# Attention: the bf16 parts of q and k are made on GpSimd, and a later group's preparation moves one tile

## The chip, the cores and the metric

The kernel runs on one core of a Trainium2 chip. The metric is the device time of one execution in microseconds (us), smaller is better. The engines are named as in the profile: PE (TensorE), DVE (VectorE), ACT (ScalarE), POOL (GpSimd) and SP, whose queue issues the DMAs.

## The reference, cut to what matters

A residual stream x of 32 tiles (128 tokens by 128 features) goes through four pairs of gated attention and gated feed-forward. Three attentions (layers 0, 1 and 3) have projections, 16 heads of width 8, and keys and values from a context of the same shape:

```python
x = x + tanh(g_xattn[0]) * L0_xattn(layernorm(x), ctx, ctx, mask, Wq, bq, Wk, bk, Wv, bv)
x = x + tanh(g_ffn[0]) * L0_ffn(layernorm(x), weight, bias)          # fp8 of x and of weight
x = x + tanh(g_xattn[1]) * L1_xattn(layernorm(x), ctx, ctx, Wq, Wk, Wv, bv, Wo, bo)
x = x + tanh(g_ffn[1]) * L1_ffn(...)                                  # 8 experts, top 2
x = x + tanh(g_xattn[2]) * L2_xattn(layernorm(x), ctx, ctx)           # 16 x 16 heads per token
x = x + tanh(g_ffn[2]) * L2_ffn(...)
x = x + tanh(g_xattn[3]) * L3_xattn(layernorm(x), ctx, ctx, mask, Wq, bq, Wk, bk, Wv, bv, Wo, bo)
x = x + tanh(g_ffn[3]) * L3_ffn(...)                                  # 8 experts, top 2
# each of L0, L1 and L3_xattn, for every tile and head:
scores = q @ k.T * 8 ** -0.5      # masked
out = softmax(scores) @ v
```

## The kernel before, in words

The 32 tiles are eight groups of four. The program has seven stages: attention 0, feed-forward 0, attention 1, feed-forward 1 with the per-token attention of layer 2, feed-forward 2, attention 2 (which is layer 3's), feed-forward 3. Every engine has its own instruction list, written out by hand in program order; semaphores (`wait_ge`) order the engines. The function `walk` unrolls the first two and the last two groups and loops over the four between.

**A group's preparation in an attention.** DVE takes the layer norm's statistics of the group's four tiles (`norm_stats`, L1171 and L1176). POOL makes the inverse deviation (`inv_std`, L447 and L449). DVE applies it (`norm`, L1194) and writes `xn`. PE turns `xn` (`turn_xn`, L815) and ACT takes it from PSUM (`take_xnT`, L635). PE then projects q, k and v one after the other through the same bank X_BANK (`project` 1 and 2, L824, and 3, L828); ACT takes q and k into the SBUF tile `area` (`take_q`, L641, and `take_k`, L646), and DVE takes v (`take_v`, L1205).

**The split.** The scores are computed with bf16 matmuls, so q and k (together 128 x 1024 fp32) are split into three bf16 parts: copy to bf16, subtract, copy, subtract, copy (`split`, L1233, L1235, L1230). The last of the five signals `split_ready`.

**The spread.** SP waits for `split_ready` and issues 18 DMAs (`spread`: six at L355 to `q_rows`, twelve at L359 to `k_rows`) that put the parts of each head onto the partitions that the matmuls contract over. `q_rows` and `k_rows` are double, by the parity of the group. After a spread SP issues the load of a later group's context (L341) and, in attention 0, of its mask (L347). The next split overwrites the parts, so it waits until the spread before it has landed (`rows_spread`).

**A tile's work.** While tile n is worked on, the scores of tile n + 1 are computed (`scores`, L845 and L847) and DVE reduces them to row maxima (`head_max`, L1220; `split_max`, L1242 and L1244). PE turns the maxima (`turn_max`, L857), computes the transposed scores less the maximum (`scores_t`, L866, L868, L873), ACT exponentiates them (L662), and PE weighs the values (`weigh`, L885). DVE normalises tile n - 1 (`normalise`, L1251, L1253, and L1256 in attention 0; `add_out`, L1261 and L1265, in the others). PE's list for tile n begins with the first scores of tile n + 1, so at the last tile of a group it begins with those of the next group, which wait for that group's spread:

```python
if j == 0:
    pe.wait_ge(rows_spread, REP * (G0[a] + group_of[0] + 1))
```

**Where the preparation of group gr + 2 stands**, while group gr with tiles t = 0 to 3 is worked on: statistics and normalising at the end of t = 0; `turn_xn` and `take_xnT` at the end of t = 1; q, then k, at t = 2; v at t = 3; and the split on DVE at t = 3, its parts between the four `head_max`. v is taken by DVE, and the mask converted, at t = 1 of the next group. In attention 0 DVE also takes the statistics of a finished group at the end of t = 2 and normalises it for feed-forward 0 at the end of t = 3 (`normed`, L1183 and L1187). Groups 0 and 1 are prepared in a start part: for attention 0 at the beginning of the kernel, for attentions 1 and 2 after the first two groups of feed-forward 0 and 2. The split of group 0 stands in it; that of group 1 stands on DVE after the first tile's maxima.

POOL has little to do in the attentions (`inv_std` only). In feed-forward 2 it also finishes the per-token products (`products`, L546, and `weighted`, L559).

## Time and profile before

| | |
|---|---|
| runs, median of 3 (lowest, highest) | 1914.92 us (1913.74, 1922.96) |
| profiled execution, span | 1906.2 us |
| between the span and the median of the runs | 8.7 us |
| mean granted TensorE clock | 0.933 of full speed |
| PE, DVE, ACT, POOL busy | 83%, 73%, 36%, 27% |

The profile gives its execution's span, from the first to the last instruction, and no other time of its own; the 8.7 us outside the span belong to every run. Sums below are made against the span and carried to the median. The two levels of TensorE's clock are 2.4 GHz (granted 1.0) and 1.2 GHz (0.5).

### The profile page before, as it was taken

To read this page: it belongs to the slowest core of one execution; us is meant where nothing else is said; L and a number is where in the kernel's file an instruction comes from. 1 tells how busy PE (TensorE), PEld (TensorE's weight loads), DVE (VectorE), ACT (ScalarE), POOL (GpSimd) and SP (SyncE) were. 2 spreads that over 40 slices of the span, in tenths; PEclk is the share of its full clock that TensorE was granted. 3 is DMA by queue.
4 is the path that set the end of the run, shared out by engine and by line. 5 is a ranking of instruction groups with operands and counts; after the bars stand their busy time and mean duration, and the time that the engine had idled before them with its cause. 6 is when DMAs were issued, how large, how long until landed. Compare 5 with 4: busy or idle time off the path is not lost. (4 is left out here: it accounts for less than half of the span.)

```text
span 1906.2 us, 36266 instructions
## 1 busy us (share of the span) xinstructions
PE 1579.4 (83%) x12360; PEld 997.5 (52%) x12360; DVE 1396.8 (73%) x3603; ACT 684.9 (36%) x1218; POOL 521.0 (27%) x565
## 2 busy tenths in 40 slices
PE   3889895388999899889889899935699899787787
PEld 1556563156666556555455555522466666444454
DVE  5777776666676446887888888876567666599997
ACT  1344443134444322333333433412344444333332
POOL 2000000000000002453543453553000000478786
PEclk9999997589999899999999999965999999899998
DMA  6453540244335000000000000004052432000000
GB/s 145 63 72 46 74 59 1 34 134 65 54 53 68 3 1 1 6 1 7 1 6 6 0 7 17 1 0 72 11 68 41 65 52 35 1 1 12 11 12 12
DMA packets 62745, 62.68 MB, mean 33 GB/s; under 512 B 6032, under 2 KB 57744, under 8 KB 62096
## 3 DMA queue, kind: packets, MB, share of 16 engines
q1 hardware_dynamic: 62608, 60.94, 20.1%
q8 instruction: 75, 1.23, 0.3%
q14 instruction: 62, 0.51, 0.1%
HBM read 21.07 MB, written 2.10 MB: 12 GB/s over the span
## 5 line engine op out<-in xcount | busy, mean ns | idle before, releaser
L662 ACT ACTIVATE probs<-bank 128x512 f32<-128x512 f32 x384 | 229.4, 598 | 357.8 <-PE bank L873 351.5
L1220 DVE TENSOR_REDUCE neg_max<-bank 128x4 f32<-128x512 f32 x384 | 260.1, 687 | 123.1 <-PE bank L847 117.5
L1020 PEld LDWEIGHTS bank<-room,area 128*128 128x128 f32 x2048 | 249.3, 195 | 102.7 <-issue 62.5
L447 POOL TENSOR_SCALAR rstd_a<-meanvar 128x4 f32<-128x4 f32 x64 | 17.0, 265 | 1042.9 <-DVE meanvar L1176 1042.9
L1020 PE MATMUL bank<-room,area 128*128 128x128 f32 x2048 | 259.5, 281 | 33.5 <-DVE area L1501 19.0
L737 ACT ACTIVATE work<-bank 128x512 f32<-128x512 f32 (+1 forms) x192 | 114.6, 597 | 356.2 <-PE bank L1045 351.2
L1049 PE MATMUL bank<-xT,room 128*128 128x512 f32 (+1 forms) x384 | 200.5, 604 | 15.5 <-DVE area L1501 15.3
L845 PE MATMUL bank<-mask_b,ident_b 128*128 128x512 bf16 x384 | 153.4, 399 | 62.7 <-DVE neg_max L1220 50.4
L1045 PE MATMUL bank<-xT,room 128*128 128x512 f32 (+1 forms) x384 | 199.2, 601 | 0.0
L1501 DVE TENSOR_TENSOR area<-work,bank 128x512 f32<-128x512 f32 (+1 forms) x192 | 128.7, 679 | 95.7 <-PE bank L1049 75.8
L559 POOL TENSOR_TENSOR prod<-mask_i,work 128x128 f32<-128x128 f32 (+3 forms) x128 | 126.5, 1021 | 155.1 <-DVE mask_i L1562 155.1
L868 PE MATMUL bank<-q_rows,k_rows 128*128 128x128 bf16 x1536 | 152.1, 223 | 0.0
L873 PE MATMUL bank<-neg_max_t,pick_max 128*128 128x128 bf16 x1536 | 151.7, 222 | 0.0
L847 PE MATMUL bank<-k_rows,q_rows 128*128 128x256 bf16 x768 | 151.6, 280 | 0.0
L868 PEld LDWEIGHTS bank<-q_rows,k_rows 128*128 128x128 bf16 x1536 | 121.2, 100 | 57.3 <-issue 10.2
L885 PE MATMUL bank<-probs,v_aug 128*32 128x128 f32 x3072 | 149.8, 287 | 1.0 <-ACT probs L662 0.7
L866 PE MATMUL bank<-ident_b,mask_b 128*128 128x512 bf16 x384 | 149.4, 389 | 0.0
L1472 DVE SCALAR_TENSOR_TENSOR x<-bank,comb,x 128x128 f32<-128x128 f32 (+1 forms) x512 | 143.0, 339 | 5.6 <-PE bank L1020 3.5
L546 POOL TENSOR_TENSOR probs<-h,work 128x128 f32<-128x128 f32 (+3 forms) x128 | 114.4, 924 | 83.1 <-DVE probs L1542 73.8
L1049 PEld LDWEIGHTS bank<-xT,room 128*128 128x128 f32 (+1 forms) x384 | 68.8, 183 | 118.0 <-issue 86.8
L1194 DVE TENSOR_SCALAR xn<-x,meanvar,rstd 128x128 f32<-128x128 f32 (+1 forms) x192 | 76.8, 463 | 57.3 <-POOL rstd L449 57.2
L873 PEld LDWEIGHTS bank<-neg_max_t,pick_max 128*128 128x128 bf16 x1536 | 104.6, 100 | 0.0
(172 smaller groups left out, 2499.8 us busy)
## 6 DMA issues: line engine op xcount, KB each, us to landing
q_rows<-area SPq DMA_DIRECT2D x144, 128.0 KB
k_rows<-area SPq DMA_DIRECT2D x288, 64.0 KB
ctxT<-ctx_t SPq DMA_DIRECT2D x24, 256.0 KB, 8.4
mask_i<-mask SPq DMA_DIRECT2D x8, 256.0 KB, 8.4
work<-ctx_in SPq DMA_DIRECT2D x8, 256.0 KB, 2.8
out<-x SPq DMA_DIRECT2D x4, 512.0 KB, 3.2
room<-w_down SPq DMA_DIRECT2D x1, 1536.0 KB, 13.7
room<-w_gate SPq DMA_DIRECT2D x1, 1408.0 KB, 6.2
```

The costliest lines, as they stand in the source:

```text
L662: act.activation(probs[j].rearrange("p a b -> p (a b)"), T_BANK[j % 2][:], ACT.Exp).then_inc(exp_done, 1)
L845: pe.matmul(dst[:], ident_b[:], bcast(mask(b, t), 4), start=True, stop=False)
L847: mm = pe.matmul(dst[:, 256 * i:256 * i + 256], q_rows[b][:, 2 * j + i, tok], k_rows[b][:, :, 2 * j + i, tok], start=False, stop=i == 1)
L866: pe.matmul(dst[:], mask(b, t), bcast(ident_b[:], 4), start=True, stop=False)
L868: pe.matmul(dst[:, i * P:(i + 1) * P], k_rows[b][:, i % 2, 2 * j + i // 2, tok], q_rows[b][:, 2 * j + i // 2, tok], start=False, stop=False)
L873: mm = pe.matmul(dst[:, i * P:(i + 1) * P], pick_max[:, 4 * j + i, :], neg_max_t[t % 2][:], start=False, stop=i == 3)
L885: mm = pe.matmul(O_BANK[32 * i:32 * i + 32, j * P:(j + 1) * P], v_aug[b][:, t, 4 * j + i, :], probs[j][:, i, :], start=True, stop=True)
L1020: mm = pe.matmul(dst[:, t * P:(t + 1) * P], h[:, t * P:(t + 1) * P], w, start=i == 0, stop=i == len(terms) - 1)
L1045: pe.matmul(S_BANK[(3 * e + c) % 2][0:size, :], wg[:, e, at:at + size], xT[b][:], start=True, stop=True).then_inc(gate_filled, 1)
L1049: pe.matmul(T_BANK[(3 * e + c) % 2][0:size, :], wu[:, e, at:at + size], xT[b][:], start=True, stop=True).then_inc(up_filled, 1)
L1220: dve.tensor_reduce(neg_max[:, 4 * j:4 * j + 4], S_BANK[j % 2][:].rearrange("p (h k) -> p h k", h=4), AX.X, ALU.max, negate=True).then_inc ...
L1472: ins = dve.scalar_tensor_tensor(xt, src[:, t * P:(t + 1) * P], comb[cb][:, t, e:e + 1], xt, ALU.mult, ALU.add)
```

## The change

DVE's `split` goes; POOL gets one of the same five instructions, with the same two waits ahead of it. On POOL the split of group 0 stands in the start part, that of group 1 directly behind (so ahead of the first tile), and that of group gr + 2 after the `inv_std` of its statistics. For attention 2 the split of group 0 stands in POOL's feed-forward 2 between the last `products` and the last two `weighted`.

The preparation of group gr + 2 stays in order but stands later: statistics still at the end of t = 0; normalising at the end of t = 1; `turn_xn`, `take_xnT` and q at t = 2; k and v at t = 3, k in the tile's first half. In attention 0 the statistics and the normalising for feed-forward 0 stand one tile earlier than before.

```diff
+            def split(p, a):
+
+                pool.wait_ge(prep_read, 4 * (G0[a] + p) + 3)
+                if positive(REP * (G0[a] + p)):
+                    pool.wait_ge(rows_spread, REP * (G0[a] + p))
+                for part in range(2):
+                    src = qk if part == 0 else qk_rest
+                    waits_apart(pool)
+                    pool.tensor_copy(parts[:, :, part, :], src).then_inc(pool_steps, ch.one())
+                    pool.wait_ge(pool_steps, ch.count)
+                    pool.tensor_tensor(qk_rest, src, parts[:, :, part, :], ALU.subtract).then_inc(pool_steps, ch.one())
+                    pool.wait_ge(pool_steps, ch.count)
+                waits_apart(pool)
+                pool.tensor_copy(parts[:, :, 2, :], qk_rest).then_inc(split_ready, 1)
+
             def attention0():
                 inv_std(1)
                 inv_std(2)
+                split(0, 0)
                 pool.wait_ge(quant_steps, 1)
...
+                split(1, 0)
...
             def attention(a):
+                split(1, a)
+
                 def body(gp, first, last, a=a):
                     for gr, b, _, left in groups(gp, first, last):
                         if left >= 2:
                             inv_std(L0[a] + gr + 3)
+                            split(gr + 2, a)
...
                 products(last + 3, 3, 1)
+                split(0, 2)
                 weighted(last + 2, 2, 1)
...
# ACT
                             exp(n, 1)
                             if left >= 2 and t == 2:
-                                take_q(gr + 2)
+                                take_xnT(gr + 2)
+                            if left >= 2 and t == 3:
+                                take_k(gr + 2)
                             exp(n, 2)
...
                             exp(n, 3)
-                            if left >= 2 and t == 1:
-                                take_xnT(gr + 2)
                             if left >= 2 and t == 2:
-                                take_k(gr + 2)
+                                take_q(gr + 2)
...
# PE
                             if left >= 2 and t == 2:
-                                project(gr + 2, b, 1)
+                                turn_xn(gr + 2)
                             if left >= 2 and t == 3:
-                                project(gr + 2, b, 3)
+                                project(gr + 2, b, 2)
                             scores_t(n, b, t, 0)
...
                             scores_t(n, b, t, 3)
-                            if left >= 2 and t == 1:
-                                turn_xn(gr + 2)
                             if left >= 2 and t == 2:
-                                project(gr + 2, b, 2)
+                                project(gr + 2, b, 1)
+                            if left >= 2 and t == 3:
+                                project(gr + 2, b, 3)
...
# DVE
-                            if splits:
-                                split(gr + 2, 0)
...
                             if t == 0 and left >= 2:
                                 norm_stats(gr + 2, xc - NT + TG * (gr + 3), x_written if a else x_loaded)
+                            if t == 1 and left >= 2:
                                 dve.wait_ge(prep_filled, 4 * (G0[a] + gr + 1) + 1)
                                 norm(gr + 2, L0[a] + gr + 2 if a or (first and b == 0) else 2 * gr + 1)
                             if a == 0 and not is_first_group(first, b):
                                 norm_count = 2 * gr + 2 if not last else 13 + b
+                                if t == 1:
+                                    norm_stats(gr - 1, TG * gr)
                                 if t == 2:
-                                    norm_stats(gr - 1, TG * gr)
-                                if t == 3:
                                     normed(gr - 1, norm_count)
```

## Rows read from the trace of the kernel before

**Rows 1.** The page: busy time, share of the span, instructions of each engine.

```profile
PE 1579.4 (83%) x12360; PEld 997.5 (52%) x12360; DVE 1396.8 (73%) x3603; ACT 684.9 (36%) x1218; POOL 521.0 (27%) x565
```

**Rows 2.** Windows, attention 0, tiles t = 0 to 3 of one group, bounded by turn_max.

```profile
core 0: us, PE busy (x) PEld busy (x) DVE busy (x) ACT busy (x) POOL busy (x), PEclk, DMA share, GB/s
120.68:127.46 6.78, 6.72 (x85) 4.44 (x86) 6.42 (x18) 3.15 (x6) 0.00 (x0) 1.00 0.74 104
127.46:138.16 10.70, 8.53 (x97) 5.71 (x89) 6.75 (x22) 3.62 (x7) 1.27 (x2) 0.84 0.80 96
138.16:146.40 8.24, 8.24 (x97) 5.06 (x89) 4.68 (x15) 4.40 (x8) 0.00 (x0) 1.00 0.28 49
146.40:154.87 8.47, 7.66 (x102) 5.18 (x93) 7.74 (x17) 3.13 (x6) 1.27 (x2) 1.00 0.01 4
```

**Rows 3.** Timeline of DVE at the end of t = 0, attention 0.

```profile
129.81 1.12 DVE L1194 TENSOR_SCALAR xn<-x,meanvar,rstd 128x128 f32 x4 [1.55 <-POOL rstd L449]
```

**Rows 4.** Windows from t = 3 of group 0 to t = 3 of group 6, attentions 0, 1, 2.

```profile
78.85:279.20 200.35, 183.17 (x2136) 119.98 (x2128) 149.23 (x392) 84.06 (x159) 15.04 (x22) 0.96 0.46 64
420.62:620.60 199.98, 185.13 (x2209) 127.08 (x2200) 139.59 (x337) 88.58 (x183) 6.33 (x10) 0.98 0.43 58
1400.29:1599.15 198.86, 184.94 (x2208) 127.06 (x2200) 139.26 (x337) 88.46 (x183) 6.33 (x10) 0.98 0.41 55
```

**Rows 5.** Timeline of SP and PE, attention 0, spread of group 7 and its first use.

```profile
258.08 3.80 SPq L355 DMA_DIRECT2D q_rows<-area  x6
261.92 7.88 SPq L359 DMA_DIRECT2D k_rows<-area  x12
...
278.22 0.38 PE L845 MATMUL bank<-mask_b,ident_b 128*128 128x512 bf16 x1 [1.70 <-issue]
```

**Rows 6.** Timeline of PE: turn_max at t = 3 of groups 5 and 6.

```profile
249.18 0.22 PE L857 MATMUL bank<-ident_b,neg_max_parts 128*32 128x128 bf16 x1
...
279.20 0.22 PE L857 MATMUL bank<-ident_b,neg_max_parts 128*32 128x128 bf16 x1
```

**Rows 7.** Timeline of SP and PE, attention 0, spread of group 0.

```profile
26.05 3.91 SPq L355 DMA_DIRECT2D q_rows<-area  x6
...
45.90 0.61 PE L845 MATMUL bank<-mask_b,ident_b 128*128 128x512 bf16 x1 [9.64 <-DMA k_rows<-area]
```

**Rows 8.** Timeline of PE and ACT: start of t = 2, and its take_q.

```profile
137.17 0.38 PE L845 MATMUL bank<-mask_b,ident_b 128*128 128x512 bf16 x1
...
141.64 0.68 ACT L641 ACTIVATE area<-bank,bq_s 128x512 f32<-128x512 f32 x1
```

**Rows 9.** Groups by line and form, DVE: the split.

```profile
L1235 DVE TENSOR_TENSOR area<-area 128x1024 f32<-128x1024 f32 x48 | 59.7, 1245 | 1.7
...
L1233 DVE CAST area<-area 128x1024 bf16<-128x1024 f32 x48 | 33.6, 701 | 7.1 <-ACT area L646 6.9
...
L1230 DVE CAST area<-area 128x1024 bf16<-128x1024 f32 x24 | 16.5, 687 | 0.2
```

**Rows 10.** Groups by line and form, POOL.

```profile
L484 POOL TENSOR_TENSOR probs<-probs,work 128x512 f32<-128x512 f32 x64 | 82.6, 1291 | 48.8 <-DVE probs L1630 48.8
...
L546 POOL TENSOR_TENSOR probs<-h,work 128x512 f32<-128x512 f32 x32 | 41.4, 1293 | 0.0
...
L546 POOL TENSOR_TENSOR probs<-h,work 128x128 f32<-128x128 f32 x32 | 18.9, 590 | 83.1 <-DVE probs L1542 73.8 <-DVE h L1194 9.3
...
L436 POOL TENSOR_SCALAR_AFFINE_SELECT pick_max<-pick_max 128x2048 bf16<-128x2048 bf16 x2 | 4.0, 2010 | 0.6 <-POOL pick_max L432 0.5
```

**Rows 11.** Timeline of POOL and DVE, start part of attention 2.

```profile
1285.93 3.81 POOL L559 TENSOR_TENSOR prod<-mask_i,work 128x128 f32<-128x128 f32 x4
...
1286.07 3.77 DVE L1194 TENSOR_SCALAR xn<-x,meanvar,rstd 128x128 f32<-128x128 f32 x4 [1.62 <-POOL rstd L449]
```

**Rows 12.** Timeline of POOL and DVE, start part of attention 2, last tokens.

```profile
1306.57 3.83 POOL L559 TENSOR_TENSOR prod<-mask_i,work 128x128 f32<-128x128 f32 x4 [4.95 <-DVE mask_i L1562]
...
1310.43 1.67 DVE L1568 TENSOR_REDUCE mask_i<-prod 128x32 f32<-128x128 f32 x4 [3.34 <-POOL prod L559]
```

**Rows 13.** Timeline of DVE, feed-forward 0 behind the start part of attention 1.

```profile
361.95 0.69 DVE L1367 TENSOR_TENSOR qb<-work 128x512 bf16<-128x512 f32 x1 [6.12 <-PE bank L986]
```

More of the change, by code:

```diff
@@ L467, in body @@
                             inv_std(count)
-                walk(pool, body, ch, 4)
+                        if not last:
+                            split(gp + b + 2, 0)
+                walk(pool, body, ch, 12)
             def attention(a):
+                split(1, a)
                 def body(gp, first, last, a=a):
@@ L537, in feed_forward0 @@
                 inv_std(18)
+                split(0, 1)
             def products(n, t, b):
@@ L1281, in attention @@
                         take_mask(0, 0)
-                    for part in range(3):
-                        split(0, part)
                     if a == 0:
@@ L1301, in attention @@
                 split_max(0)
-                for part in range(3):
-                    split(1, part)
                 def body(gp, first, last, a=a, xc=xc):
@@ L1325, in body @@
                                 head_max(n + 1, 2)
-                            if splits:
-                                split(gr + 2, 1)
                             if has_next:
@@ L1330, in body @@
                                 split_max(n + 1)
-                            if splits:
-                                split(gr + 2, 2)
                             if has_prev and a > 0:
@@ L1658 @@
 PHASES = 7
-DVE_PER_TRIP = (32, 26, 26)
+DVE_PER_TRIP = (24, 18, 18)
 def laid_out(i):
```

16 lines of the change are left out of this document (1 added, 15 removed).

## The prediction

> **What bounds the kernel now.** I read the page's first part, then the windows tile by tile in one attention, then the timelines at the places where PE stands still. The page says that PE is the busiest engine, DVE the next, and that POOL is free for most of the span [rows 1]. In the three attentions that is too coarse. Cut at each `turn_max`, the four tiles of a group take 6.78, 10.70, 8.24 and 8.47 us, 34.2 together [rows 2]. The first has no preparation work on PE and is nearly all PE. In the second, PE is busy for 8.53 of 10.70 us and its clock falls to 0.84: DVE works through statistics, a wait of 1.55 us for POOL's inverse deviation, 1.12 us of normalising [rows 3], then v and the mask, while PE has nothing. The third is all PE (the projections of q and k). The fourth holds DVE's split: DVE 7.74 of 8.47 us. Group 6 of each attention has nothing to prepare and is shorter.
>
> A second chain runs beside the engines, and the change touches it everywhere: k taken, split, 18 DMAs, first scores of the next group. SP begins the spread of group 7 at 258.08 and is issuing until 269.8; PE starts the first scores on those rows at 278.22, after standing still for 1.70 us [rows 5]. So from a finished split to the first scores is 20.1 us. The first spread of the kernel says the same from an empty DMA queue: 26.05 to 45.90, 19.9 us, and there PE waits for the DMA by name [rows 7]. In the period that ends there, `turn_max` of t = 3 went from 249.18 to 279.20, 30.0 us [rows 6], because group 6's engines were quick enough that the rows came last. Call R the moment at which PE starts the first scores at t = 3, 0.98 us ahead of that `turn_max`. R was 248.2, the spread began at 258.08: 9.9 + 20.1 us = 30.0 is what this chain needs now. The engines need 34.2, so it is hidden by about 4 us in every full group.
>
> **The change part by part.** What leaves DVE: five instructions per group, 2 x 1.245 + 2 x 0.701 + 0.687 = 4.6 us, in 24 groups 110 us busy [rows 9]. Only what lies on the path counts. Moving the normalising to the end of t = 1 takes the wait for POOL and 1.12 us out of the second tile. That tile then has statistics, v and mask ahead of its maxima, about the 2.5 us that the first tile carries today (a last split part and `normed`) at 6.78, so I give it 6.9: 3.8 us less. PE's order puts `turn_xn` and q on the third tile and k and v on the fourth, 2.1 us each where it was 2.1 and 1.0; I give both 8.3. The engines alone would then need 6.8 + 6.9 + 8.3 + 8.3 = 30.3 us per group.
>
> But the other chain grows at two places. First, k is now taken at t = 3, behind the second exponential. The same slot holds `take_q` at t = 2 today: PE starts that tile's first scores at 137.17 and q is in SBUF at 141.64 + 0.68 = 142.32 [rows 8], so k is there at R + 5.2 (today it is there before `turn_max`, at R + 0.9). Second, POOL does the split. It begins when k is there; it can't begin earlier on q, since one wait covers both. What it costs, called D: a two-input instruction of 512 elements takes 1.29 us [rows 10]; doubled it is 2.6, and by the slope of line L546 (0.59 us at 128, 1.293 at 512, so 0.70 per 384) 1024 elements take 1.293 + 512 x 0.70 / 384 = 2.2. I take 2.4, twice. No row shows POOL copying fp32 to bf16. The nearest one-input row, 2048 bf16 elements in 2.01 us [rows 10], gives 1.0 us for 1024 as the lower bound; a two-input instruction, 2.4 us, is the upper. The copy is nearer to the first, so 1.3, three times. With 0.5 for five waits and starts, D = 4.8 + 3.9 + 0.5 = 9.2 us, from 7.8 (2 x 2.2 + 3 x 1.0 + 0.4) to about 12.8.
>
> The GPSIMD Engine Reference of the Trainium skill, section "Performance versus the Vector engine", calls GpSimd the wrong choice for elementwise work and has 4497 ns for a two-input add of 2048 elements; an estimate from it is 2.25 us for 1024, inside my two bounds. Its best-case loop of 1.8 cycles an element at 1.2 GHz would make a copy of 1024 elements 1.5 us, by which D would be 9.8. The sum stays with 9.2.
>
> So the chain needs 5.2 + 9.2 + 20.1 + 0.1 = 34.6 us per period, more than the engines' 30.3: it is the bound, and PE stands still for some 4 us at every t = 3. Behind that first scores matmul PE's whole list is queued, and behind PE the exponentials, `take_k`, and so the next split: the wait is in the loop and can't be made up. Today's stall of about 2 us in the second tile brings the clock to 0.84 over 10.70 us, which is 3.4 us at 1.2 GHz [rows 2]. A 4 us stall just ahead of the 5.2 us from R to `take_k` will likely do it there; fully inside that stretch 3.4 us at half speed cost 1.7 us, outside nothing; I take 0.8. The period is 35.4 us.
>
> **The sum.** In each attention the stretch from t = 3 of group 0 to t = 3 of group 6 holds six such periods. Before: 200.35 + 199.98 + 198.86 = 599.2 us [rows 4]. After: 18 x 35.4 = 637.2. Difference +38.0. Note that the last of the six costs most, 30.0 to 35.4, since its spread had no cover.
> - Attention 0, up to t = 3 of group 0: its first split is on the path of PE's first scores: + (9.2 - 4.6). The split of group 1 begins when the first spread has landed, 45.9 + 4.6 = 50.5, and its rows are there at 50.5 + 9.2 + 20.1 = 79.8, `turn_max` at 80.8 against 78.85: +2.0 in all.
> - Attentions 1 and 2, group 0: the split of group 1 is done ahead of the first tile, as POOL is free, so its rows don't bind; the second tile's 3.8 us go, and the first tile loses its five DVE splits (on its path for some 1.5 us by the nearest case, the split tile's 8.47 against 6.78): about -5 each, -10.
> - Feed-forward 0: DVE loses 4.6 us of split but then waits 6.12 us for PE anyway [rows 13], and PE's and ACT's second preparation waits for POOL's split (`take_q` needs `split_ready`). Hidden by that wait: 0, between -4.6 and +5.
> - Feed-forward 2: POOL's split stands ahead of the last two `weighted`. The first of them ran at 1306.57, as soon as DVE had its probabilities, and DVE waited 3.34 us for it [rows 12]. DVE gets there 4.6 us earlier but POOL is 9.2 us later: +4.5, and the rest of the stage is behind it.
> - The moves in attention 0 of the statistics for feed-forward 0, and ACT's changed order: same instructions, in tiles that now have 4 us to spare: 0. If the periods were not bound by the spread, they would be in the 30.3 above.
>
> Sum: 38.0 + 2.0 - 10 + 0 + 4.5 = +34.5 us. Span 1906.2 + 34.5 = 1940.7, with the 8.7 us outside it 1949.4: about 1949 us.
>
> **Rivals.**
> *The copies are cheap and the clock holds.* D = 7.8 and nothing for the clock: period 33.2, 18 x 33.2 = 597.6, so -1.6, then -0.8 (attention 0's start) - 10 + 3: about -9 us, 1906 us. For it: the lower bounds are both rows of POOL. Against: two sides must be at their bounds together. Everything between this and D = 8.3 is no change.
> *The spread does not pace, and the removed stall pays* (the other side). If POOL split in 5 us or less, or the 20.1 us shrank by 4, the periods were the engines' 30.3 to 30.7: 18 x 30.7 = 552.6, -46.6, and with the -10 of the groups 0 about -57: 1858 us. It decides at D + spread = 25. For it: removing the stalled tile is real, 3.8 us of 34. Against: 5 us is below what two two-input instructions and three copies take by any POOL row, and two spreads, one into an empty queue, agree on 20 us.
> *POOL and DVE hold each other up.* While POOL ran four instructions from 1285.93 to 1289.74, DVE's normalising of four tiles took 3.77 us, and ended with them [rows 11], where it takes 1.12 otherwise [rows 3]. POOL's split now runs over t = 3 and t = 0, where DVE has `split_max`, and L1256 or L1265, with both inputs in SBUF. If three such in each of two tiles wait on average half of a 2.4 us instruction, DVE loses 7 us in a group, more than its room, and if POOL waits in turn D grows by 1.5 to 2: period 37.1, +68.6 + 5 - 10 + 6 = +70: 1985 us. For it: these rows. Against: DVE's maxima (L1220) read PSUM and are most of its work, and POOL pauses between its five instructions. The page SBUF — State Buffer of the Trainium skill, section "Who interferes with whom", has it as an exclusive lock between a GpSimd instruction and a DVE instruction in a two-port mode or with two SBUF inputs; the trace agrees, with 3.77 against 1.12 us.
>
> **How the numbers follow.** This kernel's runs can tell about 0.5%, 9.6 us, from no change. The forecast case (D from 8.3 to 11, 1925 to 1990) has 0.57, the mutual hold-up 0.13, cheap copies 0.15 (of that 0.12 within 0.5%, 0.03 faster), no pacing 0.15. Faster 0.18, same 0.12, slower 0.70. The upper end takes D = 11.2 (copies of 1.9 us) and 1.2 for the clock: period 37.8, 81 + 6 - 10 + 6 = +83: 1998. The lower end goes to the cheap copies and a little under, 1900; what is left out is mostly the case at 1858. Given the likeliest case alone the range is 1925 to 1990.
>
> **What the profile after should show.** Three copies of about 1.3 us and two subtractions of about 2.4 on POOL in each of 24 groups; L845 waiting for the DMA of `k_rows`, or standing idle, for about 4 us once per group at t = 3; `turn_max` at t = 3 every 35 us; the second tile down to about 7 us with no wait for `rstd`; the clock's dip at t = 3 and no longer in the second tile; the last of the six periods longer by 5 us. The prediction is wrong if a split takes under 7.5 us from `take_k` to SP's first issue, if the spread takes clearly less than 20 us, or if k is taken earlier than R + 4.

## The result, and the profile after

The changed kernel takes 1929.74 us (median of nine runs, 1922.24 to 1935.64). The kernel before, run beside it, takes 1913.12 (nine runs, 1910.38 to 1922.96). The ratio is 1.0085, 95% interval 1.0066 to 1.0104, so it is slower by 16.6 us. The prediction was 1949, 35 more than before: the direction is right, and half of the size.

The profiled execution of after has a span of 1933.8 us and took 1935.64, so 1.8 us lie outside the span. Before's profiled span of 1906.2 is therefore one of an execution near 1908, some 5 us under its median, and after's is 6 us above its own. The two traces differ by 27.6 us, where the medians differ by 16.6. This has to be kept in mind where stages are compared. It also means that the 8.7 us, which were taken ahead of the prediction as time outside the span in every run, are mostly the distance of one quick execution from the median; in the traces taken since, 1.7 to 2.1 us lie outside.

First the page's busy times of after, which answer to [rows 1]:

```profile
PE 1595.6 (83%) x12360; PEld 1004.5 (52%) x12360; DVE 1327.0 (69%) x3483; ACT 684.0 (35%) x1218; POOL 696.7 (36%) x685
```

The split has moved as planned: 120 instructions fewer on DVE, 120 more on POOL. DVE is busy 70 us less, where the split had been 110 [rows 9], so its other instructions have become 40 us longer. POOL is busy 176 us more, and PE 16 us more at the same number of matmuls: its work did not grow, its clock was lower for longer (0.923 in the mean, 0.933 before).

Then the windows of after, each from t = 3 of group 0 to t = 3 of group 6, in attentions 0, 1, 2 (columns as in [rows 2]), to set beside [rows 4]:

```profile
85.82:296.82 211.00, 188.17 (x2136) 121.06 (x2130) 133.53 (x366) 84.58 (x160) 58.35 (x52) 0.94 0.44 61
437.17:638.04 200.87, 187.14 (x2211) 127.13 (x2202) 120.44 (x307) 89.11 (x184) 50.55 (x40) 0.98 0.42 57
1426.45:1624.53 198.08, 186.91 (x2211) 127.19 (x2202) 120.36 (x307) 88.98 (x184) 50.55 (x40) 0.98 0.40 56
```

DVE does 16 to 19 us less in each, and it buys nothing: a period (from t = 3 of one group to t = 3 of the next, the mean of six) is 35.2, 33.5 and 33.0 us where it was 33.4, 33.3 and 33.1. The windows tile by tile, in a group of attention 1, show what took the place:

```profile
478.82:485.68 6.86, 6.86 (x96) 4.79 (x88) 4.31 (x11) 3.36 (x7) 3.27 (x3) 1.00 0.25 51
485.68:492.55 6.87, 6.87 (x97) 4.79 (x88) 5.81 (x20) 3.32 (x7) 1.26 (x2) 1.00 0.90 99
492.55:503.46 10.91, 8.54 (x102) 5.54 (x94) 5.59 (x16) 4.50 (x9) 0.00 (x0) 1.00 0.56 77
503.46:512.08 8.62, 8.62 (x106) 5.98 (x98) 4.70 (x10) 3.90 (x8) 4.03 (x3) 1.00 0.01 3
```

The tile of 10.70 us in [rows 2] (9.8 to 11.2 in attention 1 before) is now 6.87, all of it PE. The window that ends with t = 3's `turn_max` has become the one of 10.91, with PE busy for 8.54. The stall has changed its tile. What ends it is in the waits (us, times, longest), of before and then of after:

```profile
DVE xn L1194 <- POOL rstd L449: 57.2, 35, 3.7
```

```profile
DVE xn L1218 <- POOL rstd L449: 28.8, 17, 3.7
...
PE bank L869 <- DMA k_rows<-area: 48.6, 16, 14.6
```

Of DVE's 35 waits for the inverse deviation 18 are gone. PE waits for the rows of k 16 times, where it was twice before. Call R, as the prediction does, the start of PE's first scores at t = 3. The timeline of SP, POOL, ACT and PE over one period of attention 1, from R to the next R, gives the whole chain:

```profile
469.21 0.38 PE L869 MATMUL bank<-mask_b,ident_b 128*128 128x512 bf16 x1 [1.85 <-DMA k_rows<-area]
...
473.67 0.68 ACT L670 ACTIVATE area<-bank,cols 128x512 f32<-128x512 f32 x1
474.51 1.04 POOL L459 CAST area<-area 128x1024 bf16<-128x1024 f32 x1 [19.12 <-ACT area L670]
...
481.27 1.04 POOL L464 CAST area<-area 128x1024 bf16<-128x1024 f32 x1
482.50 3.79 SPq L355 DMA_DIRECT2D q_rows<-area  x6
486.33 7.87 SPq L359 DMA_DIRECT2D k_rows<-area  x12
...
502.46 0.39 PE L869 MATMUL bank<-mask_b,ident_b 128*128 128x512 bf16 x1 [1.87 <-DMA k_rows<-area]
```

From R = 469.21 to k in SBUF (473.67 + 0.68 = 474.35) are 5.1 us; the split ends at 481.27 + 1.04 = 482.31, 8.0 us later; SP's first issue to PE's next first scores are 20.0. With 0.2 us between split and issue that is 33.25 = 502.46 - 469.21. Every microsecond of this period lies on the chain, as predicted; its second link is 8.0 us and not 9.2. In 17 of the 18 periods PE stands still ahead of the first scores, for 1.1 to 5.3 us; in one, of 31.2 us in attention 2, it does not.

In all periods of attention 0, in two of attention 1 and in two of attention 2 the first link is longer. The windows from R to the moment at which k is taken, one of attention 0 and two of attention 1:

```profile
119.85:126.63 6.78, 6.78 (x59) 3.84 (x60) 2.05 (x5) 2.52 (x5) 0.00 (x0) 0.75 0.04 13
469.21:474.36 5.15, 5.15 (x59) 3.22 (x60) 1.93 (x4) 2.52 (x5) 0.00 (x0) 1.00 0.00 0
535.67:542.50 6.83, 6.83 (x59) 3.94 (x60) 1.93 (x4) 2.53 (x5) 0.00 (x0) 0.75 0.00 0
```

The same 59 matmuls take 6.8 us at a granted clock of 0.75, and 5.15 at 1.00. PE had stood still just before in all three, for 3.6, 1.85 and 1.80 us. In the first and the third the clock fell to its lower level (1.2 GHz) for part of what followed, in the second it stayed at 2.4 GHz. The links of the 18 periods, added up from such timelines:

| link | forecast | measured | difference |
|---|---|---|---|
| R to k taken, with the clock | 18 x 6.0 = 108.0 | 111.1 | +3.1 |
| k taken to SP's first issue | 18 x 9.3 = 167.4 | 146.5 | -20.9 |
| SP's first issue to the first scores | 18 x 20.1 = 361.8 | 352.4 | -9.4 |
| 18 periods | 637.2 | 610.0 | -27.2 |

Where the 27.6 us between the two traces lie, by stretches bounded by `turn_max` and by the beginning of feed-forward 2 (a group 0 counts from its first to its last `turn_max`):

| stretch | before | after | difference | predicted |
|---|---|---|---|---|
| attention 0 to t = 3 of group 0 | 78.8 | 85.8 | +7.0 | +2.0 |
| 18 periods | 599.2 | 610.0 | +10.8 | +38.0 |
| groups 0 of attentions 1 and 2 | 55.8 | 43.6 | -12.2 | -10 |
| feed-forward 0 | 86.8 | 91.8 | +5.0 | 0 |
| feed-forward 2 | 126.7 | 133.0 | +6.3 | +4.5 |
| feed-forward 1 and 3, ends of attentions | 958.9 | 969.7 | +10.9 | 0 |

The first five rows sum to +16.7, the difference of the medians. The last row is code that the change did not touch but for the end of attention 0, which is 0.5 us longer. Feed-forward 1 took from 597.1 to 611.5 us over the traces of this study, with the same instructions; this pair has 598.2 and 606.3. That scatter is most of what makes the pair of traces wider than the pair of medians.

### The profile page after: what moved, and what is told of

Read it like the earlier page. It is cut to its first block and busy times, and to the rows that moved or that the text cites. A ratio compares the mean times of both kernels' runs of the same rounds, so it can differ in the third digit from the quotient of the medians.

```text
span 1933.8 us, 36319 instructions
## 1 busy us (share of the span) xinstructions
PE 1595.6 (83%) x12360; PEld 1004.5 (52%) x12360; DVE 1327.0 (69%) x3483; ACT 684.0 (35%) x1218; POOL 696.7 (36%) x685
## 5 line engine op out<-in xcount | busy, mean ns | idle before, releaser
L1073 PE MATMUL bank<-xT,room 128*128 128x512 f32 (+1 forms) x384 | 203.4, 612 | 15.5 <-DVE area L1500 15.3
L1069 PE MATMUL bank<-xT,room 128*128 128x512 f32 (+1 forms) x384 | 202.6, 610 | 0.0
L459 POOL CAST area<-area 128x1024 bf16<-128x1024 f32 x48 | 50.3, 1048 | 377.2 <-ACT area L670 339.4
L461 POOL TENSOR_TENSOR area<-area 128x1024 f32<-128x1024 f32 x48 | 102.7, 2140 | 11.5 <-issue 7.7
```

The lines of the kernel that those rows point to most:

```text
L1069: pe.matmul(S_BANK[(3 * e + c) % 2][0:size, :], wg[:, e, at:at + size], xT[b][:], start=True, stop=True).then_inc(gate_filled, 1)
L1073: pe.matmul(T_BANK[(3 * e + c) % 2][0:size, :], wu[:, e, at:at + size], xT[b][:], start=True, stop=True).then_inc(up_filled, 1)
```

## The experiments

The theory: the chain of late k, POOL's split and spread paces the periods, so moving the preparation saves a stall and lets k come too late to profit from it, and the split on POOL adds its length to the chain one for one. Rivals: POOL's instructions hold DVE's up and so lengthen the tiles; DVE's shorter list or POOL's split alone makes the loss, whatever the order; the clock's fall is the loss. Beside them stood two open places, the start of attention 0 and the ends of feed-forward 0 and 2. Each ratio is to the kernel before as run beside the experiment, whose median was 1911.1 to 1913.4 us.

### 1. The split on POOL alone

The kernel before, with POOL's split as in the change and none on DVE; the preparation stands where it stood.

```diff
 # POOL: split(0, a), split(1, a), split(gr + 2, a) as in the change
 # DVE, t == 3:
-                            if splits:
-                                split(gr + 2, 0)
```

> The kernel before with one part of the change: all splits on GpSimd (same five instructions), the order of the preparation as before, so k is in SBUF before turn_max of t = 3. Theory 1 (the chain k taken, split, 18 DMAs, first scores of the next group sets the period once k is taken late): here that chain needs 0.9 + 8.0 + 20.1 = 29.0 us and stays hidden; the second tile keeps its 10.7 us; the group takes 33 to 34 us, no wait for the rows but in group 6. With 8 to 12 us lost in the start of attention 0 and in feed-forwards 0 and 2, where GpSimd's splits stand in DVE's way, the time is within 10 us of before. Theory 2 (what costs is GpSimd itself: its instructions hold DVE up in the tiles t = 3 and t = 0): then the periods are above 34.2 us and the time is above before by as much as the whole change, 15 us or more.

Measured: 1926.16 us, ratio 1.0073 (1.0047 to 1.0099). The windows of the three stretches:

```profile
88.75:288.10 199.35, 180.80 (x2134) 118.92 (x2128) 136.56 (x361) 84.00 (x159) 56.77 (x52) 0.97 0.47 64
431.65:632.39 200.74, 187.97 (x2209) 128.63 (x2200) 118.88 (x307) 88.54 (x183) 50.38 (x40) 0.97 0.42 57
1421.72:1621.30 199.58, 186.80 (x2209) 127.93 (x2200) 118.92 (x307) 88.41 (x183) 50.38 (x40) 0.97 0.41 55
```

The six periods of each attention stay within 1.1 us of [rows 4], with 13 to 21 us less busy time on DVE. So DVE's split in the fourth tile cost next to no time: DVE's 7.74 us of 8.47 [rows 2] fitted beside PE's 7.66, and the tile of t = 3 takes 8.0 us here against 8.2 before in attention 1, and 8.4 against 8.3 in attention 0 (means of five groups). The busy time shows the hold-up too. Six splits of 4.58 us are 27.5 us; DVE is relieved of 12.7, 20.7 and 20.3 only, so its other instructions take 6.8 to 14.8 us more in six periods, 1.1 to 2.5 us in a group. PE's work hides it. The total was expected within 10 us of before and came 15 over it. What is slower in this kernel lies outside the periods: the start of attention 0 (88.8 us to t = 3 of group 0 against 78.9), feed-forward 0 (91.5 against 86.8) and feed-forward 2 (133.2 against 126.7).

### 2. The order alone

After's order with the split back on DVE.

```diff
 # DVE, split removed from POOL
                                 head_max(n + 1, 2)
+                            if left >= 2 and t == 3:
+                                split(gr + 2, 0)
                             if has_next:
                                 head_max(n + 1, 3)
                                 split_max(n + 1)
+                            if left >= 2 and t == 3:
+                                split(gr + 2, 1)
+                                split(gr + 2, 2)
```

> The other part alone: the preparation one tile later as in the change, the split on DVE, its first copy and subtraction between the third and fourth head_max of t = 3 and the rest behind split_max. Theory 1: k is in SBUF 5.2 us after the first scores of t = 3, the split is ready at about 11.5 to 12.5, so the period is 31.7 to 32.7 us where before has 33.3 in the mean: -10 to -30 us over 18 periods and about -4 for each group 0, so 1875 to 1895. PE waits about 1 us for the rows at t = 3. Theory 2 (GpSimd's instructions in the tiles cost, the chain does not): the periods are the engines' 30.5 to 31 us, 50 us under before.

Measured: 1883.38 us, ratio 0.9843 (0.9791 to 0.9896). The three stretches:

```profile
77.33:267.73 190.40, 176.80 (x2139) 116.08 (x2130) 150.66 (x397) 84.64 (x160) 14.23 (x22) 1.00 0.49 67
410.19:601.57 191.38, 184.74 (x2210) 126.19 (x2202) 138.33 (x337) 89.16 (x184) 6.33 (x10) 1.00 0.45 60
1385.36:1574.92 189.56, 184.41 (x2210) 126.16 (x2202) 137.65 (x337) 89.04 (x184) 6.34 (x10) 1.00 0.42 58
```

The reorder alone is worth 27.9 us in the periods (571.3 against 599.2), with k as late as in the change. A period is 31.7 us, and the clock is 1.00 throughout. DVE's split takes 6.5 us from k taken to its end here, and 5.1 + 6.5 + 20 is 31.6. In attention 0 PE stands still ahead of the first scores in all six periods (0.9 to 3.5 us), so the chain paces there too, with a shorter link. In attention 1 PE's waits for the rows of k (us, times, longest) are only

```profile
PE bank L845 <- DMA k_rows<-area: 1.9, 2, 1.7
```

and in attention 2 it has none. There the chain and the engines' own work come out level: a full period of 31.9 us in attention 1 is also what the kernel of experiment 4 with the split on DVE takes, where k is early. POOL's split instead of DVE's costs 609.95 - 571.34 = 38.6 us in the periods; 26 of it are the longer split (8.1 us from k taken to SP's first issue, against 6.7), and 18 the first link, which is 5.15 us in every period here and was longer in ten of 18 there, at the lower clock. The spread gives 5 back (352 against 357 in all), and the last period of attention 2 another 1.4, by where its `turn_max` falls.

### 3. A longer and a shorter split on POOL

After, with one more copy, and with one subtraction less, in groups 2 to 7.

```diff
 # one more copy, in split:
+                    pool.tensor_copy(parts[:, :, 2, :], qk_rest).then_inc(pool_steps, ch.one())
+                    pool.wait_ge(pool_steps, ch.count)
 # one subtraction less, in split:
+                    if part == 1 and less:
+                        continue
```

> The whole change with one more copy (of the third part, the same data again) in GpSimd's split of groups 2 to 7 of each attention, 18 in all, 1.1 us each with its wait. Theory 1 (the chain k taken, split, spread sets the period): every period is 1.1 us longer, so the stretch from t = 3 of group 0 to t = 3 of group 6 is 6.7 us longer in each attention (217 to 218, 207 to 208, 204 to 205 us where the change has 211.0, 200.9, 198.1) and the time 20 us above the change. Theory 2 (the engines' own work sets it, GpSimd is beside the path): no difference.

> The whole change with the second subtraction left out of GpSimd's split of groups 2 to 7 (the third bf16 part is then a copy of the first remainder), 2.2 us less each. Theory 1: the periods shrink by 2.2 us until the engines' own need of about 31 us binds, so the stretch of six goes from 211.0 to 196 to 198, from 200.9 to 188 to 189 and from 198.1 to 187 to 188, some 35 us less in all. Theory 2: no difference beyond 2 us a stretch.

Measured: the longer one 1959.4 us (ratio 1.0247, 1.0216 to 1.0277), the shorter one 1884.52 (0.9845, 0.9813 to 0.9876). The three stretches of the longer one, then those of the shorter one:

```profile
85.14:305.15 220.01, 190.35 (x2138) 121.59 (x2130) 133.60 (x366) 84.57 (x160) 64.61 (x58) 0.91 0.41 58
446.73:659.76 213.03, 192.62 (x2211) 129.69 (x2202) 120.34 (x307) 89.11 (x184) 56.80 (x46) 0.95 0.38 54
1444.03:1649.26 205.23, 188.67 (x2211) 128.00 (x2202) 120.48 (x307) 88.99 (x184) 56.81 (x46) 0.98 0.38 54
```

```profile
85.24:273.40 188.16, 178.24 (x2138) 116.71 (x2130) 130.90 (x366) 84.58 (x160) 45.57 (x46) 0.99 0.50 68
414.08:599.70 185.62, 183.11 (x2210) 125.88 (x2202) 119.86 (x307) 89.11 (x184) 37.78 (x34) 1.00 0.45 62
1387.66:1573.04 185.38, 183.00 (x2210) 125.87 (x2202) 119.71 (x307) 88.98 (x184) 37.79 (x34) 1.00 0.44 59
```

1.12 us more per split is 6.7 us in six periods. The stretches grew by 9.0, 12.2 and 7.2, and the time by 30 us where 20 were expected. The chain theory holds as to sign and place, and is short in size; the clock gives the rest: added up over the 18 periods, the first link (R to k taken) is 9.3 us longer than in the change, 5.5 of them in attention 1, where the clock fell from 0.98 to 0.95 as PE's stalls grew. So a longer stall costs more than itself. On the other side, 2.25 us less per split (a subtraction and its start) is 13.5 us in six periods, and the stretches shrank by 22.8, 15.3 and 12.7 to a period of 31 us. PE is then busy for 183 of 185.5 us in attentions 1 and 2: the engines' own need, predicted as 30.3 us, is about 31, and it was hidden under the chain by some 2 us. The three stretches fell by 50.8 us where 35 were expected; most of the excess is in attention 0, where the clock rose from 0.94 to 0.99.

### 4. k early, the normalising late

Experiment 1 with one block moved: DVE's normalising stands between the second `head_max` and `normalise` at t = 1, and PE's and ACT's lists are those of before, so that k is taken at the end of t = 2.

```diff
 # DVE
                                 head_max(n + 1, 1)
+                            if t == 1 and left >= 2:
+                                dve.wait_ge(prep_filled, 4 * (G0[a] + gr + 1) + 1)
+                                norm(gr + 2, ...)
...
                             if t == 0 and left >= 2:
                                 norm_stats(gr + 2, ...)
-                                dve.wait_ge(prep_filled, 4 * (G0[a] + gr + 1) + 1)
-                                norm(gr + 2, ...)
```

> All splits on GpSimd, the order as before but for the normalising of group gr + 2, which stands between the second head_max and normalise of t = 1 and no longer at the end of t = 0; turn_xn, q, k and v as before. Theory 1: the stall of the second tile goes and the chain keeps its 29.0 us, so both are under the engines' need: period 30 to 30.7 us, 18 x -3 = -50 us, less some 10 us for the feed-forwards and the start: 1865 to 1880. Theory 2: DVE is held up in t = 3 and t = 0, the period stays above 32 us and the time above 1890.

Measured: 1885.0 us, ratio 0.9861 (0.9815 to 0.9908). The six periods take 183.4, 186.9 and 186.9 us, 42.1 less in all than before and 52.8 less than after, with the same split on POOL. Its length is no loss as soon as k is early, so POOL's split is not slow in itself: it is slow where it stands. That also speaks against a mutual hold-up of POOL and DVE in the periods that costs time, which would be the same here. The total was expected at 1865 to 1880 us, with 50 us less in the periods and 10 more outside them; it is 42 less and some 16 more.

Outside the periods this kernel still has POOL's losses: 34.1 us for group 0 of attention 0 (28.1 before), 91.5 and 132.4 for feed-forward 0 and 2. Two more kernels take them away: the kernel before with this one move and the split left on DVE, and the same with only groups 2 to 7 of each attention split on POOL.

```diff
 # the second of the two, POOL
                         if not last:
+                            split(gp + b + 2, 0)
...
                             inv_std(L0[a] + gr + 3)
+                            split(gr + 2, a)
 # no split(0, a) and split(1, a) on POOL: these stay on DVE
```

> The kernel before with one edit: the normalising of group gr + 2 stands between the second head_max and normalise of t = 1 instead of at the end of t = 0. Splits stay on DVE, k is taken where it was. The chain of k, split and spread needs 29.9 us as before, the engines 30 to 31. So the stretches of six become 183 to 188 in attention 0 and 187 to 190 in the others (200.3, 200.0, 198.9 before), and as nothing stands on GpSimd in the start and in feed-forwards 0 and 2, nothing is lost there: 1911 - 16 - 12 - 11 - 3 x 2 = about 1865 us. If GpSimd's taking the splits were what made the tiles of the version with all splits on GpSimd short, the stretches would be 192 or more here.

> The normalising in the middle of t = 1 as in the best version so far, the splits of groups 0 and 1 of each attention on DVE as before, those of groups 2 to 7 on GpSimd. Theory 1: both chains are under the engines' need, so taking 4.6 us per group off DVE gives what DVE's split still cost in the tile t = 3: by the two versions seen, 183.4 against 186.3, 186.9 against 189.0 and 186.9 against 188.0 in the stretches of six, so about 6 us under the version with all splits on DVE: 1862 to 1868 us. Feed-forward 0 takes 87 and feed-forward 2 127 us, as before (91.5 and 132.4 with all splits on GpSimd). If GpSimd's splits hold DVE up in the attentions' tiles, it is not faster than the version with all on DVE.

Measured: 1870.88 us (ratio 0.9786, 0.9764 to 0.9809) and 1865.8 us (0.9749, 0.9717 to 0.9780). The latter is the fastest kernel of the study, 48 us under before and 64 under after. Its three stretches:

```profile
80.59:264.03 183.44, 175.12 (x2136) 116.31 (x2128) 132.35 (x361) 84.08 (x159) 57.47 (x52) 1.00 0.51 70
402.27:589.50 187.23, 183.00 (x2208) 125.83 (x2200) 118.70 (x307) 89.12 (x183) 50.43 (x40) 1.00 0.45 62
1369.95:1557.23 187.28, 182.91 (x2209) 125.82 (x2200) 118.62 (x307) 89.00 (x183) 50.42 (x40) 1.00 0.43 59
```

The other, expected at about 1865 us, has 186.3, 189.0 and 188.0 there. So once neither chain nor stall binds, taking the split from DVE is worth 5.3 us over the three attentions by this pair of traces (the two ratios' intervals still touch). Little more can be had: PE is busy for 98% of the time that is left in attentions 1 and 2.

### 5. The start of attention 0

The timeline of POOL in after, behind the all-reduce, and the rows of line L461 by source:

```profile
34.64 0.38 POOL L472 PARTITION_ALL_REDUCE s<-s  x1 [5.53 <-DMA k_rows<-area]
49.59 1.04 POOL L459 CAST area<-area 128x1024 bf16<-128x1024 f32 x1 [14.57 <-issue]
58.36 2.12 POOL L461 TENSOR_TENSOR area<-area 128x1024 f32<-128x1024 f32 x1 [7.73 <-issue]
```

```profile
L461 POOLq MODIFY_POOL_CONFIG  x2: 11/11/11, 50.7 to 50.7; - x2
```

In the middle of the split of group 1 POOL does nothing for 7.7 us, and a change of its configuration stands at the start of the hole. In before the same kind of entry came at 36.4 us, directly behind the all-reduce, and POOL had nothing to do until 60.73. The reading was that POOL loads code for the next kind of instruction, called the reload here. Two kernels were made: one puts a tiny product of two constants directly behind the all-reduce, which should take the reload there; one puts 96 empty instructions ahead of POOL's first, to see whether the hole depends on where the code lies.

```diff
                 pool.partition_all_reduce(...).then_inc(amax_all, 1)
+                pool.tensor_tensor(s1[:, 15:16], minus_half[:, 0:1], minus_half[:, 1:2], ALU.mult).then_inc(pool_steps, ch.one())
+                pool.wait_ge(pool_steps, ch.count)
                 split(1, 0)
 # the other kernel, at the start of POOL's list
+            for _ in range(96):
+                pool.nop(nofuse=True)
```

> The whole change with one tiny GpSimd product (one element a partition, into an unused column) right behind the all-reduce of the start part. In the trace after, the list of GpSimd has a MODIFY_POOL_CONFIG at 29.1 for the all-reduce and another at 50.7, between the first copy and the first subtraction of the split of group 1, and 7.7 us of nothing there. If loading the code of the two-input operation is what takes them, the load now happens at about 35 us, while the first spread is in flight: the hole goes, the first t = 3 comes 5 to 7.7 us earlier (up to group 0's t = 3: 23.5 to 26 us instead of 31.4), and nothing else changes. If the hole comes from the transfers that have just landed, it stays.

> The whole change with 96 empty instructions in front of GpSimd's list. In the four traces with all splits on GpSimd there is a hole of 6.9 to 7.7 us between the first copy and the first subtraction of the split of group 1 in attention 0, in which nothing is awaited. If the hole comes from where GpSimd stands in its list (its next instructions have to be fetched), it moves to another place or goes. If it comes from the data or from the 18 transfers just landed, it stays where it is.

Measured: 1924.52 us with the product (ratio to before 1.0049, 1.0024 to 1.0073; after had 1.0085). POOL's timeline:

```profile
42.22 0.18 POOL L473 TENSOR_TENSOR s<-minus_half 128x1 f32<-128x1 f32 x1 [7.09 <-issue]
49.64 1.04 POOL L459 CAST area<-area 128x1024 bf16<-128x1024 f32 x1 [7.24 <-DMA k_rows<-area]
50.76 2.13 POOL L461 TENSOR_TENSOR area<-area 128x1024 f32<-128x1024 f32 x1
```

The 7.1 us of standing still are now ahead of the product, where POOL waits anyway, and the split runs through. Group 0 of attention 0, from its first to its last `turn_max`, takes 24.9 us where it took 31.4. This place is settled by its trace: 6.5 us. That the medians fell by 5.2 agrees, though the two intervals overlap. The kernel with the empty instructions took 1935.99 us in one run with the hole as it was; its profile has the same 36319 instructions as after's, so the empty ones left no trace in it, and it says nothing. That the standing still is a loading of code is an inference; what is shown is that it comes at the first two-input instruction behind the all-reduce and moves with it.

### 6. The end of feed-forward 0

The split of group 1 stands first in POOL's list for attention 1, free to run while feed-forward 0 still works. The timeline of DVE and POOL in after, at its end:

```profile
394.58 1.35 POOL L459 CAST area<-area 128x1024 bf16<-128x1024 f32 x1 [20.00 <-DMA k_rows<-area]
...
396.00 2.54 POOL L461 TENSOR_TENSOR area<-area 128x1024 f32<-128x1024 f32 x1
...
396.48 2.35 DVE L1354 TENSOR_SCALAR work<-room,s 128x512 f32<-128x512 f32 x1
...
398.86 1.14 DVE L1356 TENSOR_SCALAR work<-work 128x512 f32<-128x512 f32 x1
399.80 2.17 POOL L461 TENSOR_TENSOR area<-area 128x1024 f32<-128x1024 f32 x1
400.03 2.22 DVE L1358 TENSOR_SCALAR work<-work 128x512 int32<-128x512 int32 x1
```

The same three instructions of DVE took 0.48, 0.43 and 0.43 us in the kernel before, the first of them here:

```profile
379.13 0.48 DVE L1355 TENSOR_SCALAR work<-room,s 128x512 f32<-128x512 f32 x1
```

In after each ends 0.3 us behind an instruction of POOL beside it. The kernel tried keeps POOL's split out of there.

```diff
             def attention(a):
+                pool.wait_ge(x_written, NT * BLOCK[a])
                 split(1, a)
```

> The whole change, but in attentions 1 and 2 GpSimd begins the split of group 1 only when the feed-forward before has written its last x. If the ends of feed-forwards 0 and 2 were longer because this split holds DVE up there (5.1 and 4.2 us by the trace after), these go; but then the rows of group 1 come 8 + 20 us after the attention's start where the engines need them after 22, so the first t = 3 comes 6 us later in each. Net against the change: between -3 and +6 us. If the ends of the feed-forwards do not get shorter, the split was not what lengthened them.

Measured: 1921.69 us, ratio 1.0046 (1.0017 to 1.0074). The window of feed-forward 0, in after and then in this kernel:

```profile
323.65:415.40 91.75, 34.04 (x197) 17.76 (x188) 60.35 (x124) 12.45 (x21) 19.81 (x17) 0.55 0.20 39
```

```profile
324.56:411.83 87.27, 33.42 (x196) 17.64 (x187) 55.80 (x124) 12.45 (x21) 18.14 (x17) 0.57 0.21 43
```

DVE runs the same 124 instructions in 4.6 us less, and the stage is 4.5 us shorter, which is the +5.0 of the table but for 0.5. Group 0 of attention 1 keeps its 21.8 us, so the delay costs nothing there, where up to 6 us in each attention had been expected. Feed-forward 2 went from 133.0 to 129.7.

## Why the prediction was right in direction and too large

The forecast difference was some 18 us too large. The 18 periods were taken 27.2 us too long (the split 20.9 and the spread 9.4 too long, the first link 3.1 too short), and the two groups 0 2.2 us. Against that some 12 us were missing in the sum, at the start of attention 0 and in feed-forwards 0 and 2.

**Right: the chain paces the periods**, 17 of 18 by PE's standing still. Its form, R to k taken, split, spread, first scores, was the forecast's, and two doses bear it out: with splits of 8.0 and 9.1 us, a period of attention 2 is 33.0 and 34.2 us, and with a split shorter by 2.25 us it stops at the engines' 31. R to k taken is 5.15 us at full clock where 5.2 was taken. The second tile fell to 6.87 us, predicted 6.9. The stall moved to the first scores of t = 3. That k is taken one tile later is what gives the gain back: k early and the same POOL split run 52.8 us faster in the periods (experiment 4).

**The step that failed: D, "9.2 us", the length of POOL's split.** POOL's rows by form in after:

```profile
L461 POOL TENSOR_TENSOR area<-area 128x1024 f32<-128x1024 f32 x48 | 102.7, 2140 | 11.5 <-issue 7.7
L459 POOL CAST area<-area 128x1024 bf16<-128x1024 f32 x48 | 50.3, 1048 | 377.2 <-ACT area L670 339.4 <-DMA k_rows<-area 20.0 <-issue 14.6
L464 POOL CAST area<-area 128x1024 bf16<-128x1024 f32 x24 | 24.9, 1037 | 3.2
```

The copies are 1.04 us and not 1.3, the subtractions 2.14 and not 2.4. Both stand at the lower bounds that the prediction worked out (1.0 and 2.2) and then left for higher values. D is 8.0, and over the 18 periods this link is 20.9 us shorter than forecast, most of what is missing. It is also less than the 8.3 us from which the forecast case was said to begin, so the time fell into that case's range partly by luck: the losses of 10 us in two places that the sum had missed (below) brought it there. The rival of cheap copies had D = 7.8 and the bet against it, that "two sides must be at their bounds together", was the error: both bounds came from rows of the same engine, and were likely to be right or wrong together. The best-case loop of the Trainium skill (GPSIMD Engine Reference, section "Performance versus the Vector engine") would give the copy an estimated 1.5 us; the row says 1.04, and the row decides.

**The spread, "20.1".** It is 20.0 us in the period shown and 19.6 to 20.3 in 14 of 18, but 17.3 to 18.8 in four, among them the last of attentions 1 and 2, so 9.4 us shorter in all. That it can be shorter was one of the prediction's own signs of being wrong; why it is in these four was not tried. The cost of "the last of the six", put at 30.0 to 35.4, came out so in attention 0 (30.0 to 35.3) and as 29.9 to 32.9 and 28.8 to 31.4 in the others.

**The clock, "I take 0.8".** Over 5.15 us the first link is 2.0 us longer in the mean in attention 0 (six of six periods), 0.5 in attentions 1 and 2 (two of six each, by 1.6 to 1.7), 18.4 us in all; with the 0.05 us by which 5.2 was too long the sum had 15.3. So the size is near, 3.1 us too small, but as the mean of unlike cases. The rival that the clock's fall is the loss is right to that extent: without it 18 of the 610 us would go. But it came only behind PE's standing still, and in the fastest kernel of experiment 4 the clock is 1.00 in all three stretches.

**Missed: the start of attention 0, "+2.0 in all".** It was +7.0. The sum held the split's length and no standing still between two of its instructions. Before's trace has the same entry behind the all-reduce, in time that nobody waited for; what was not asked is where the cost would fall once POOL has work behind the all-reduce. With it out of the way (experiment 5) the stretch is 79.2 us, +0.4.

**Missed: feed-forward 0, "Hidden by that wait: 0".** It was +5.0, at the end of the range given. The wait for PE [rows 13] does hide the start part's split. The loss was a second split, that of group 1, which the prediction placed "ahead of the first tile, as POOL is free" and did not look at what DVE was doing there. The rival of POOL and DVE holding each other up was thus right in kind and wrong in place and size: in the tiles DVE loses 1.1 to 2.5 us per group where the rival had 7, less than its room there, and POOL loses almost nothing (its subtractions take 2.12 at the least and 2.14 in the mean); in feed-forward 0 it costs 4.5 us of time, and in feed-forward 2 3.3.

**Feed-forward 2, "+4.5".** It was +6.3, and the near hit is luck, since the one term of the sum was half as large and another was missing. The late `weighted` is there, with a long wait of DVE for it:

```profile
1338.17 1.67 DVE L1567 TENSOR_REDUCE mask_i<-prod 128x32 f32<-128x128 f32 x4 [10.86 <-POOL prod L582]
```

It begins 66.5 us into the stage; in before [rows 12] it was 64.3, so this costs 2.2 us and not 4.5. The missing term is the split of group 1, as in feed-forward 0. The last normalising of the stage, in before and in after:

```profile
1356.53 1.12 DVE L1194 TENSOR_SCALAR xn<-x,meanvar,rstd 128x128 f32<-128x128 f32 x4 [1.62 <-POOL rstd L449]
```

```profile
1384.45 4.41 DVE L1218 TENSOR_SCALAR xn<-x,meanvar,rstd 128x128 f32<-128x128 f32 x4 [1.62 <-POOL rstd L449]
```

Beside POOL's split it takes 3.3 us more. Experiment 6 takes the split away from there: this normalising is back at 1.12 us, and the stage is 3.3 us shorter. The last 0.8 us were not traced to a cause.

**The groups 0, "about -5 each".** They were -6.5 and -5.7. In attention 1 the first tile gained 2.7 us and the second 3.9; in attention 2, where the second tile had no long stall before (8.45 us), the first gained 4.2 and the second 1.6. The sum of -10 was near, its parts fit attention 1 only.

**The other side, "18 x 30.7".** The engines' own need, which that rival had at 30.3 to 30.7 us, is 30.9 in the shorter split of experiment 3 and 30.6 to 31.2 in the fastest kernel. That the fourth tile would gain next to nothing by the loss of DVE's split was right as well (experiment 1); with k and v in it, it is 8.6 us at full clock, where 8.3 was taken. Together they say why the change could not win: what was to be had lay in the stall of the second tile, 28 us by experiment 2 and 36 by the kernel of experiment 4 that leaves the split on DVE, and after's order pays for it with the time at which k is taken.

## What to carry to other kernels

When preparation work is moved later to get a stall out of the way, ask which long transfer hangs on its last product, and move the consumer of the stall instead: here the normalising alone, moved by half a tile, brought 36 us over the periods of three attentions, while the whole preparation moved by a tile brought 28 and, with a slower splitter, cost 11. An engine that looks free is free only per place: its work stands on the path at the starts of stages, and beside DVE's SBUF-to-SBUF work it costs DVE's time as well as its own. And a stall that recurs in a loop should be costed twice, with the clock kept and with the clock lost, since the same stall of 1.8 us did both in this kernel. Last, where two bounds of a cost come from rows of one engine, they should not be counted as two independent chances.

## What the runs showed of the hardware

- After a PARTITION_ALL_REDUCE, POOL's next two-input instruction waited 7.7 us (7.1 for the product of experiment 5), with a MODIFY_POOL_CONFIG in front. A CAST between the two did not wait and did not bring the reload. The Trainium skill has a loading time of about 6 us for the first call of freshly loaded code (GPSIMD Engine Reference, section "Instruction dispatch"); 7.1 and 7.7 us are of that order, and if it is that loading, it is paid again here: the same subtraction had run before the all-reduce, at 22.4 us.
- DVE instructions with one fp32 or int32 input of 128 x 512, from SBUF to SBUF, took 2.35 and 2.22 us beside a POOL subtraction, against 0.48 and 0.43 alone; POOL's first subtraction there took 2.54 us against 2.12. Four normalisings of 128 x 128 took 4.41 us against 1.12. In the tiles of the attentions, where most of DVE's work reads PSUM, all its instructions together lose 1.1 to 2.5 us in a group with one split of 8.0 us.
- Three fp32 to bf16 copies and two subtractions of 128 x 1024 take 8.0 us on POOL and 6.5 us on DVE as placed in experiment 2. For the copies alone it is 1.04 us against 0.69 to 0.70, and for the subtractions 2.14 against 1.25.
- The same standing still of PE left the granted clock at 1.00 or brought it to 0.75 over the next 6.8 us, within one attention. In attention 1 of the change, 1.85, 1.87 and 1.94 us were each followed by 1.00 (5.15 us for the 59 matmuls), 1.80 and 2.01 us by 0.75 (6.8 us); in attention 2, 1.6 and 2.1 us by 1.00, 1.9 and 2.0 us by 0.75. In attention 0, 2.4 us and more were followed by 0.62 to 0.76 each time. The length alone does not decide at 1.8 to 2.1 us; what does stays open.
